# Constants of later phases loaded during the stem, and their preparation moved to the offset phase

## What is computed

```python
h = conv2d(x, stem_w, stem_b, 4)                  # patches of 4x4: 96 channels, 24x24 pixels
h = leaky_relu(batchnorm(h, bn1_g, bn1_b, bn1_m, bn1_v))
offset = conv2d(h, off_w, off_b, 4)               # 16 taps x 2, 6x6 positions
h = deform_conv(h, offset, dcn_w, dcn_b)          # bilinear samples, then 192 channels
h = leaky_relu(batchnorm(h, bn2_g, bn2_b, bn2_m, bn2_v))
# as tokens: 36 an image; 128 text rows from a table quantized to 8 bits join them
h = h + attention(layernorm(h))                   # 12 heads of 16, window of 64 to either side
h = h + kan(kan(layernorm(h), w1), w2)            # cubic B-splines with 16 control points, hidden width 512
```

## Time and profile before

| | us |
|---|---|
| median of 3 runs | 2579.64 |
| lowest and highest | 2578.28 and 2585.09 |
| the profiled execution | 2577.04 |
| its span in the profile | 2575.3 |
| TensorE busy | 2380.9 (92%) |
| VectorE busy | 1921.8 (75%) |
| ScalarE busy | 1407.6 (55%) |
| POOL busy | 213.1 (8%) |

### The profile page before, as it was taken

One profiled execution on the slowest core, in us unless ns is written; L12 is line 12 of the kernel. 1 busy time (PEld: TensorE's weight loads), 2 busy tenths in 40 slices (PEclk: granted clock), 3 DMA queues, 4 the chain that ended last, 5 costly groups with the idle time before them and its releaser, 6 DMA issues.

```text
span 2575.3 us, 50122 instructions
## 1 busy us (share of the span) xinstructions
PE 2380.9 (92%) x20297; PEld 2212.2 (86%) x20297; DVE 1921.8 (75%) x2505; ACT 1407.6 (55%) x1391; POOL 213.1 (8%) x132
## 2 busy tenths in 40 slices
PE   8959985899999981999999999999999999999999
PEld 6736675777777871999999999999999999999999
DVE  7849942566666643876767676768999999999995
ACT  2229831344444434534344443558888888788881
POOL 2202210000000002121212121100000000000000
PEclk9989997899999995999999999999999999999999
DMA  3435524011111110000000000021000000000000
GB/s 111 132 85 149 147 67 158 24 44 43 43 43 43 41 39 25 15 19 25 18 25 18 25 18 25 22 98 49 22 21 26 24 21 21 21 24 25 21 17 9
DMA packets 99887, 116.36 MB, mean 45 GB/s; under 512 B 15575, under 2 KB 90983, under 8 KB 99047
## 3 DMA queue, kind: packets, MB, share of 16 engines
q1 hardware_dynamic: 81571, 93.41, 12.1%
q0 software_dynamic: 3616, 10.54, 1.6%
q10 hardware_dynamic: 14596, 10.83, 1.4%
HBM read 83.88 MB, written 30.86 MB: 45 GB/s over the span
## 4 chain that ended last, share of the span: by engine, by line
PE 59%; DVE 1%; issue 1%; DMA 0%; POOL 0%; ACT 0%; SPq 0%; POOLq 0%; DVEq 0%
PE spline_acc L1750 25%; PE spline_acc L1723 9%; PE spline_acc L1722 9%; PE spline_acc L1724 9%; PE spline_acc L1744 5%; PE spline_acc L1746 2%; PE spline_xT L1703 0%; DMA spline_x<-h_scr 0%; DVE spline_weights_low L1405 0%; DVE spline_xn L569 0%; DVE spline_f L1443 0%; DVE spline_b L1421 0%; DVE spline_t L1426 0%; DVE spline_b L1415 0%; DVE spline_a L1410 0%
## 5 line engine op out<-in xcount | busy, mean ns | idle before, releaser
L1750 PE MATMUL spline_acc<-spline_weights,spline_f 128*128 128x192 f32 x3936 | 671.9, 328 | 0.0
L1750 PEld LDWEIGHTS spline_acc<-spline_weights,spline_f 128*128 128x128 f32 x3936 | 637.1, 190 | 0.0
L1722 PE MATMUL spline_acc<-spline_f,spline_weights_high 128*128 128x328 f32 x1536 | 480.0, 312 | 7.2 <-DVE spline_f L1443 7.2
L1723 PE MATMUL spline_acc<-spline_f,spline_weights_high 128*128 128x328 f32 x1536 | 482.8, 314 | 0.0
L1724 PE MATMUL spline_acc<-spline_f,spline_weights_low 128*128 128x328 f32 x1536 | 476.4, 310 | 0.0
L1443 DVE SCALAR_TENSOR_TENSOR spline_f<-spline_n,spline_a 128x984 fp32r<-128x984 f32 x128 | 151.1, 1180 | 200.1 <-PE spline_acc L1724 198.4
L1722 PEld LDWEIGHTS spline_acc<-spline_f,spline_weights_high 128*128 128x128 f32 x1536 | 290.1, 189 | 7.4 <-issue 7.4
L1723 PEld LDWEIGHTS spline_acc<-spline_f,spline_weights_high 128*128 128x128 f32 x1536 | 289.1, 188 | 0.0
L1724 PEld LDWEIGHTS spline_acc<-spline_f,spline_weights_low 128*128 128x128 f32 x1536 | 288.9, 188 | 0.0
L1454 DVE SCALAR_TENSOR_TENSOR spline_f<-spline_n,spline_b 128x1536 f32<-128x1536 f32 x164 | 287.0, 1750 | 0.0
L1744 PE MATMUL spline_acc<-spline_weights_split,spline_f_high 128*128 128x384 f32 x656 | 218.2, 389 | 8.2 <-issue 8.2
(11 more groups left out here) (197 smaller groups left out, 4108.6 us busy)
## 6 DMA issues: line engine op xcount, KB each, us to landing
sample_pos<-pos_scr SPq DMA_DIRECT2D x32, 540.0 KB, 4.3
hid_scr<-spline_hid SPq DMA_DIRECT2D x64, 164.0 KB, 1.8
spline_xn<-hid_scr SPq DMA_DIRECT2D x41, 256.0 KB, 3.0
attend_spread<-rec_scr SPq DMA_DIRECT2D x128, 61.5 KB, 2.1
pix_scr<-stem_by_pixel SPq DMA_DIRECT2D x32, 225.0 KB, 2.5
sample_h<-pix_scr POOLq DMA_DIRECT2D x32, 225.0 KB, 4.3
spline_weights_raw<-w SPq DMA_DIRECT2D x1, 6144.0 KB, 23.6
spline_weights<-w SPq DMA_DIRECT2D x4, 1536.0 KB, 5.9
```

The source lines that it names most:

```text
L1722: nc.tensor.matmul(z, high, x_high, start=start, stop=False)
L1723: nc.tensor.matmul(z, high, x_low, start=False, stop=False)
L1750: last = nc.tensor.matmul(z, f_rest[i][:, cols], w2[:, i, r, :], start=False, stop=stop)
```

## The change

A class `Constants` is added. It owns the tiles and semaphores of constants that several phases use, among them one identity for all phases, and lists 14 loads: off_w (192 KB), off_bias, off_grid (144 KB), identity (64 KB); pix_neg, wq (576 KB), wk (576 KB), wv (288 KB); rest_low, mask (492 KB), piece (123 KB), pick (123 KB); minus_low, dcn_w (1152 KB). ScalarE issues them in the stem, four behind each of images 0 to 2 and two behind image 3. The deform weights go into the space that the spline weights take later.

In the offset phase ScalarE splits the projection weights, POOL sets the ones, VectorE forms the diagonals, casts and subtracts, and TensorE runs the four spread products behind the convolution; VectorE copies them behind the position add. The sample, deform and attend phases lose these loads and steps. The output weights wo are still loaded in the attend phase, behind the token rows of pairs 0 and 1, and TensorE waits for them ahead of the first pair.

```diff
 # stem_phase, ScalarE
             for u in range(4):
                 image(0, u, True)
+                for dst, src, done in c.loads[4 * u:4 * u + 4]:
+                    act.dma_start(dst, src).then_inc(done, 16)
 # offset_phase
-            sp.dma_start(w[0:C1, :, :], off_w).then_inc(weights_in, 16)
-            sp.dma_start(bias[:, :], off_vec).then_inc(weights_in, 16)
-            sp.dma_start(base[:, :], grid).then_inc(weights_in, 16)
             sp.wait_ge(pos_ready, 1)
...
+        @block.scalar
+        def _(act):
+            act.wait_ge(c.attend_in, c.attend_count)
+            for raw, high, low in zip(c.raw, c.high, c.low):
+                nc.scalar.activation(high[:], raw[:, 0:2, :], ACT.Copy).then_inc(w_high, 1)
+                nc.scalar.activation(low[:, 1, :], raw[:, 2, :], ACT.Copy).then_inc(w_high, 1)
+
+        @block.gpsimd
+        def _(pool):
+            pool.memset(ones[:], 1.0).then_inc(ones_set, 1)
+            pool.wait_ge(ones_set, 1)
+            pool.memset(c.ones_row[D1:P, :], 1.0).then_inc(ones_set, 1)
+
         @block.tensor
         def _(pe):
-            pe.wait_ge(weights_in, 48)
+            pe.wait_ge(c.offset_in, 64)
...
             last.then_inc(conv_done, 1)
+            pe.wait_ge(ones_set, 1)
+            pe.wait_ge(diag_ready, 4)
+            for j in range(4):
+                last = nc.tensor.matmul(spread[:, j * C1:(j + 1) * C1], ones[0:C1, :], diag[0:C1, j, :],
+                                        start=True, stop=True)
+            last.then_inc(spread_ready, 1)
 
         @block.vector
         def _(dve):
-            dve.wait_ge(weights_in, 48)
+            dve.wait_ge(c.offset_in, 64)
+            # four diagonals; casts of ones, piece, mask and pick; six subtractions of the low parts
             dve.wait_ge(conv_done, 1)
             # the position add
+            dve.wait_ge(spread_ready, 1)
+            nc.vector.tensor_copy(c.rows[:], spread[:, 0:2 * D].rearrange("p (j d) -> p j d", j=2)
+                                  ).then_inc(rows_ready, 1)
+            dve.wait_ge(rows_ready, 1)
 # sample_phase, SyncE
-            sp.dma_start(neg[0:PIXC, :], pix_neg).then_inc(const_in, 16)
 # deform_phase
-            sp.dma_start(ident[:], ident_in).then_inc(ident_here, 16)
-            sp.dma_start(w[0:C1, :, :], dcn_w).then_inc(vectors_in, 16)
...
-            # POOL's ones, VectorE's diagonals and copy, TensorE's spread products
-            pe.wait_ge(vectors_in, 16)
+            pe.wait_ge(c.dcn_in, 16)
 # attend_phase, SyncE
-            for dst, src in loads:
-                sp.dma_start(dst[:], src).then_inc(const_in, 16)
             for u in range(2):
                 load(sp, x[u], x_in[u], u)
+            sp.dma_start(wo[:], a["wo"]).then_inc(wo_in, 16)
             sp.dma_start(w_raw[:], a["w1"].rearrange("p i (h r) o -> p (i h) (r o)", h=2)).then_inc(w1_in, 16)
...
-            # ScalarE's and VectorE's splits, VectorE's casts, all waits for const_in, consts and w_low
 # attend_phase, TensorE
+            pe.wait_ge(wo_in, 16)
             pair(0, 0, first=True)
```

206 lines of the change are left out of this document (102 added, 104 removed).

## The result

| us | before | after |
|---|---|---|
| median, measured side by side | 2582.69 (8 runs, 2577.14 to 2593.74) | 2571.70 (8 runs, 2567.68 to 2574.68) |
| the profiled execution | 2577.04 | 2573.99 |
| its span | 2575.3 | 2572.3 |
| mean granted clock in it | 0.967 | 0.965 |

The ratio is 0.9951, with a 95% interval from 0.9932 to 0.9971: the kernel is faster by 0.5%. The forecast was 2560.6 us, range 2550.5 to 2569.5; the median lies outside it. Of the 19 us that were expected, 11 came, as the two medians measured side by side tell it.

The account below looks back on a forecast made before the run. TensorE's spline phase holds most of the time, untouched; the change acts on idle phase starts. -3.4 - 0.4 - 10.6 - 7.0 + 2.4 = -19.0 us from 2577.04 gives 2558.0, plus 2.6 for a median: 2560.6 us, range 2550.5 to 2569.5.

Parts of the forecast that it names:

- Offset phase: Convolution starts at the phase's opening, about 146.2 instead of 149.62, since its weights are already there: -3.4 us.
- the pixel table's -0.4: Sampling phase: SyncE's load of the pixel table, ahead of the position loads in its queue, goes: -0.4 us.
- The covers: Offset phase: splits and casts fit beneath the 16.10 us convolution, spread products and copy beneath SyncE's outputs: zero cost.
- Sampling phase: Only the pixel table's load goes, -0.4 us; no other change in the phase was forecast.
- Deform phase: First product at 358.3, not 368.94: -10.6 us, 7.8 from the loads and 2.8 from the clock being at 1.00.
- Attention start: Normalization begins at 420.8 instead of 427.85, waiting for pair 0's token load, not POOL's memsets: -7.0 us.
- Stem: 14 loads added on ScalarE's queue delay patch loads by their traffic; issue time is covered: +2.4 us.
- a link: Stem: a patch delay that adds up, one in three images; two among images 3 to 6, 0 to 3.6 us together.
- the extreme of 8: Stem: upper end in us if single issues on ScalarE's queue also stall; as a rival 2566.2, chance 0.08.
- the case that free queues cost nothing: Stem: patch packets pass between the added loads, so nothing is lost; 2.4 us less than the forecast sum.
- The rival of ScalarE's stalled queue: Stem: 10 following issues stall up to 3.20 us each, 25.9 us lost with contention, 2584.1, slower; chance 0.02.
- Pair 0: Attention: stays near 37 us; rivals, clock rises earlier (2554.7) or a second pair at the lower level (2566.5), chance 0.12 each.

Follow-up runs that it names:

- stem_loads_only: The kernel before with the same 14 loads added on ScalarE's queue in the stem, into tiles nobody reads: 2593.21 us, ratio to before 1.0027.
- dcn_late: The changed kernel with the deform weights loaded in the sampling phase, four pieces on ScalarE's queue, instead of the stem: 2572.14 us, ratio to before 0.9954.
- the combined kernel: The changed kernel with early loads spread, pair 0's token load in pieces, pair 1 normalized earlier and idle TensorE products: 2555.56 us, ratio to before 0.9903.

## Why the prediction was wrong

**Offset phase: right.** Convolution at 152.21, the opening; -3.4 was forecast, and with the pixel table's -0.4 the stretch is 3.8 us shorter. The covers held: splits ended at 157.1 of a convolution that ran to 168.4, spread products took 1.1 us, half of it beneath SyncE's outputs. Nothing there was mis-sized.

**Sampling phase: nearly right.** The phase itself is longer by 0.9 us (182.1 from the first position load to the opening of the deform phase before, 183.0 after), which I had at zero. Its cause wasn't sought; the changed kernel's second profile has 182.5, and it lies within what profiles of unchanged sampling code differ by.

**Deform phase: right,** -10.7 us from the opening to the first product, forecast -10.6, the clock's 2.8 among it: VectorE has its first product 5.5 us behind the start of the products, not 8.3. The experiment that puts the load back costs 10.3 us in that phase.

**Attention start: right,** -6.75, forecast -7.0: late next was the token load and not POOL, and the load took 7.4 us, as the steady row had it. The issues of the loads behind it did stall (1.63 and 2.79 us on SyncE's queue), with nobody behind them who was late.

**Stem: the first step that failed, in its size.** The term was 1.2 us a link, two links, +2.4. It measured +6.05, and +6.5 alone. I took the price of a 225 KB load beside 540 KB of another queue (1.8 us more) and moved downward from it, since a patch load is half as large. The mechanism, bytes beside a patch load and two links, is what the profile shows, but the links measured 4.0 and 1.3 us. The row I priced from had 540 KB beside its load; here 1.44 MB lay in the queue, 2.7 times as much, and the patch landed 4.0 us late in a single link (24.59 against 20.60). That the price goes by what lies in the queues at the issue fits this and the 9.8 us of the loads ahead of image 0; no series of sizes was run. My 3.6 us for contention alone was no upper bound; only the extreme of 8, which I had put down to stalls of ScalarE's queue that did not occur, held it. One stall did occur, 1.29 us of SyncE's queue, which I had not thought of. The Trainium skill says that queues of different engines share the same DMA engines ("DMA: Bandwidth & Descriptors", "Issuing engines are not separate DMA queues"); the trace agrees, and the case that free queues cost nothing is refuted by +6.5.

**The rival of ScalarE's stalled queue** did not come: ScalarE's issues in the stem took 0.33 to 0.59 us each, as SyncE's did, not 3.06.

**Pair 0: the step that failed most.** I took pair 0 at 36.8 us, from one execution, as what the changed kernel would do, "the work of that stretch is the same, in the same order", and gave 5.9 us either way with 0.12 each. It took 46.6 and 40.7 us in two profiles, +9.8 and +3.9. Both the chance and the price were too small: the price supposed that the worst is one more pair at the lower level, when pair 0 itself could run at the lower level almost throughout. In seven profiles of kernels whose attention code is the changed one, unaltered or with only the token load cut, the stretch from normalization to pair 2 took 104.0 to 109.9 us, against 100.1 to 100.2 in three of four profiles with the code of before. The other side of it is that the code of before can be long too: stem_loads_only has 45.5 us for pair 0 and 111.0 for the stretch, in an execution of 2594.82 us at a mean clock of 0.962. So 5.9 us are shown to differ between executions of one program. Whether the 3.8 us between the shortest stretch of the one code and the usual one of the other are the change's doing isn't shown: all three short profiles of the code before are from executions at a clock of 0.967.

Summed: forecast -19.0; stem +3.6 more than forecast, sampling phase +0.9, pair 0 +9.8 in the first profile: -4.7, where pair 2 starts 4.6 us earlier. With +3.9 for pair 0, the second profile (its stem and sampling phase add 3.5 and 0.4): -11.2, where that execution measured 2566.09 - 2577.04 = -10.95.

**The base.** The median of the three runs shown was 2579.64; larger sets (7, 8, 17, 23 and 24 runs) gave 2583.31, 2582.69, 2579.15, 2586.17 and 2584.45. The medians in the same measurement differ by 11.0 us; against them, not against 2579.64, the gain has to be read. So 3.1 us of the miss of 11.1 are not the change's: the base of the forecast was a median of three, and the gain itself fell short by 8.0.

**What stays open.** Why the attention code finds its lower clock longer in the changed kernel's timing in most profiles isn't settled. The experiments on it moved the places where the clock falls, and none held it through pair 0; what makes it fall or rise there is open. Whether the kernel before's executions of 2585 us and more have a long pair 0 was never seen in a profile of that kernel, only in the one of stem_loads_only; that their mean clock is 0.960 to 0.962 against 0.965 to 0.968 speaks for it, that five stay over 2585 us with idle products and clocks of 0.964 to 0.966 leaves room for another cause.

## What to carry to other kernels

When loads are moved forward beside other work, price them by the bytes that lie in the queues when the next short load is issued, and ask of the phase that takes them in how late its own loads already are: 1.15 MB cost 1.1 to 2.0 us in one phase and 4.8 to 4.9 in another, and saved 10.3 at the place they came from. Where a stretch of the profile runs at the lower clock, its time is one draw: take a second profile, or give it a range as wide as the whole stretch at either level, and look at which of its timed executions, by their mean clock, the profiled one belongs to. Removing a wait for many loads makes the last remaining load the next thing to improve, and its shape can matter more than its size.

## What the hardware showed

- A 108 KB load that lands in 2.4 us took 6.4 us with 1.44 MB issued ahead of it by another engine and 0.74 MB behind it, and 9.8 when all 3.7 MB had been issued ahead of it. The same 14 transfers with the same 1943 packets and almost no bytes cost 0.5 to 1.2 us in all, against 6 to 6.5.
- An issue on SyncE's queue took 1.29 us instead of 0.34 while 1152 KB issued by ScalarE were under way; in the changed kernel's second profile it was 1.41, in stem_loads_only 1.44, and 0.35 in the kernel without that load in the stem (dcn_late).
- A token load in pieces of 36, 46 and 82 rows was there after 7.4 us; in pieces of 36, 32, 14, 80 and 2 rows after 3.6 us, with the same bytes and two issues more.
- The same program had pair 0 in 46.6 and in 40.7 us, by one further fall of the granted clock to 0.50 for 17 us. The Trainium skill ("TensorE: Matmul & The Clock Gate", "What's actually happening") calls the number of slow products at a kernel's start run-variable. Here the difference is a later fall, in the middle of a kernel, so the page is a neighbouring case; the two profiles lie 5.9 us apart.
- TensorE was busy for 20.77 of 21 us at a granted clock of 0.50 before it rose (after, 451 to 472), and for 8.97 of 9 us in the kernel before (465 to 474).
- Idle TensorE products held the clock at 1.00 through the first scores (428 to 444), and it fell in the next gap, in which TensorE waited for VectorE. That was 2 us behind the first exponential (442.29). With that gap closed it still fell: 4 us behind the first exponential with both changes and in the combined kernel, 18 us behind it in the combined kernel with the deform weights in the sampling phase. From the normalization to pair 2 it took 106.6 us with the gap closed, 96.9 with idle products, 100.0 with both and 94.0 and 97.2 in the combined kernels, against 104.0 to 109.9 with neither: shorter in each profile, but not a sum, and with idle products alone four of seven executions were no faster than the changed kernel's.
